# Recurrence outputs and input reloaded earlier, six of eight batches gated and summed before the last batch's feed-forward

## What is computed

```python
xn = layernorm(x)                                  # [8, 256, 128]
s  = recurrence(xn)                                # linear recurrence over the 256 tokens of each batch
y  = xn
for i in range(6):                                 # 6 layers, 16 heads of 64, windows of 32
    y = local_attention(shift(y), Wqkv[i], ...) @ Wo[i] + y
    y = feed_forward(shift(y), ln_g[i], ln_b[i], W1[i], b1[i], W2[i], b2[i]) + y
out = x + s * silu(y)
```

## Time and profile before

| what | value |
|---|---|
| median of 3 runs | 1658.5 us (1656.65 to 1660.97) |
| profiled execution, its own time | 1657.53 us |
| its span, first to last instruction | 1655.7 us (1.83 us less) |
| mean granted TensorE clock | 0.990 of full speed |
| busy share PE / DVE / ACT / POOL | 95% / 86% / 67% / 74% |

### The profile page before, as it was taken

One profiled execution on the slowest core, in us unless ns is written; L12 is line 12 of the kernel. 1 busy time (PEld: TensorE's weight loads), 2 busy tenths in 40 slices (PEclk: granted clock), 3 DMA queues, 4 the chain that ended last, 5 costly groups with the idle time before them and its releaser, 6 DMA issues.

```text
span 1655.7 us, 75427 instructions
## 1 busy us (share of the span) xinstructions
PE 1567.6 (95%) x31996; PEld 1312.3 (79%) x31996; DVE 1416.7 (86%) x2757; ACT 1109.9 (67%) x1980; POOL 1231.0 (74%) x1200
## 2 busy tenths in 40 slices
PE   4889999999999999999999999999999999999995
PEld 2468888788888788888888888888888877888884
DVE  4698899889889988988988898989889888888963
ACT  4265777776677777667776766777676776767663
POOL 2377788878778887877887787787778887777851
PEclk9799999999999999999999999999999999999998
DMA  3033223333223323322333322333323333322222
GB/s 112 22 92 73 66 72 81 92 79 86 69 68 73 101 69 89 74 72 68 93 79 82 82 70 69 94 78 82 82 67 73 84 86 82 83 68 66 71 64 81
DMA packets 109742, 127.96 MB, mean 77 GB/s; under 512 B 52064, under 2 KB 55648, under 8 KB 109152
## 3 DMA queue, kind: packets, MB, share of 16 engines
q1 hardware_dynamic: 109408, 123.13, 29.5%
HBM read 20.27 MB, written 2.10 MB: 14 GB/s over the span
## 4 chain that ended last, share of the span: by engine, by line
PE 62%; DVE 12%; ACT 11%; issue 7%; POOL 6%; DMA 1%; SPq 0%; DVEq 0%; POOLq 0%; ACTq 0%
PE F L529 10%; PE O L634 9%; PE VTb L542 7%; PE S L559 6%; PE QKb L500 6%; PE F L599 4%; PE QKb L502 4%; PE QKb L501 4%; DVE t L882 4%; PE S L580 3%; ACT L773 3%; ACT hid L773 2%; DVE mx L910 2%; POOL t L1052 2%; PE S L552 2%
## 5 line engine op out<-in xcount | busy, mean ns | idle before, releaser
L1052 POOL TENSOR_TENSOR t<-t 128x512 f32<-128x512 f32 x384 | 492.2, 1282 | 193.6 <-DVE t L882 180.4
L882 DVE TENSOR_TENSOR t<-QKb,table 128x1024 f32<-128x1024 f32 x384 | 468.3, 1220 | 61.5 <-ACT sq L713 59.4
L1027 POOL TENSOR_TENSOR t<-t,rn 128x512 f32<-128x512 f32 x384 | 401.3, 1045 | 128.5 <-DVE rn L939 128.4
L713 ACT ACTIVATE sq<-QKb 128x512 f32<-128x512 f32 x384 | 231.2, 602 | 238.0 <-PE QKb L502 232.6
L634 PEld LDWEIGHTS O<-PT,V 64*64 64x64 f32 x12288 | 198.6, 134 | 57.5 <-issue 55.3
L634 PE MATMUL O<-PT,V 64*64 64x32 f32 x12288 | 218.4, 220 | 15.9 <-DVE rn L939 15.8
L891 DVE TENSOR_REDUCE ss<-sq 128x16 f32<-128x1024 f32 x192 | 232.0, 1209 | 0.0
L542 PE MATMUL VTb<-cst,t 128*128 128x128 f32 x1536 | 230.5, 272 | 0.1
L529 PEld LDWEIGHTS F<-wo_sb,OT 128*128 128x128 f32 x1536 | 200.5, 191 | 16.3
L1034 POOL TENSOR_TENSOR E<-E,rs 128x512 f32<-128x512 f32 x192 | 200.4, 1044 | 14.6 <-DVE rs L904 14.6
L542 PEld LDWEIGHTS VTb<-cst,t 128*128 128x128 f32 x1536 | 185.4, 141 | 31.1 <-POOL t L1027 2.8
(11 more groups left out here) (152 smaller groups left out, 2769.3 us busy)
## 6 DMA issues: line engine op xcount, KB each, us to landing
V<-v_tok SPq DMA_DIRECT2D x1440, 64.0 KB, 2.0
w_raw<-in_wqkv SPq DMA_DIRECT2D x36, 256.0 KB, 3.0
wo_sb<-in_wo SPq DMA_DIRECT2D x6, 512.0 KB, 4.1
xs<-xm SPq DMA_DIRECT2D x48, 64.0 KB
xs<-xm SPq DMA_DIRECT2D x48, 63.5 KB
w_sb<-in_w SPq DMA_DIRECT2D x6, 341.0 KB
w_sb<-in_w SPq DMA_DIRECT2D x6, 192.0 KB, 3.8
y_spill<-OT SPq DMA_DIRECT2D x1, 1024.0 KB, 4.2
```

Source lines behind the costliest of these rows:

```text
L713: act.activation(sq[:, v % 4, :], QK_ps, ACT.Square).then_inc(sq_done, 1)
L882: dve.tensor_tensor(t12[:, v:9 + v % 4:8 + v % 4 - v, :].rearrange("p c (h d) -> p c h d", h=8), QK_ps.rearrange("p (h d) -> p h d", h=8). ...
L1027: pool.tensor_tensor(w, w, rn[:, vv // 4, 8 * (vv % 4):8 * (vv % 4 + 1)].unsqueeze(2) .to_broadcast([P, 8, DH]), ALU.mult).then_inc(qk_nor ...
L1052: pool.tensor_tensor(w, w, t12[:, 8 + v % 4, :].rearrange("p (h c d) -> p h c d", h=8, c=2)[:, :, ::-1, :], ALU.add).then_inc(add_done, 1)
```

## The change

The recurrence's output is read back into `sq` and not into `V[:, 1]`, which allows it from slot 4 of step 48 on. The reload of x moves to slot 0 of step 49. ACT applies silu to six batches in slot 2 of step 50, and DVE multiplies and adds these six in slot 5 of step 50, after it has finished batch 6 (step 46). Two batches are left for the end. The transposes stay where they were, and so do all operations in number, except that ACT loads its function table two times more.

```diff
+Y_LOAD, X_LOAD = STEPS * SLOTS + 4, STEPS * SLOTS + 8
+EARLY, GATED, MIXED = B - 2, STEPS * SLOTS + 18, STEPS * SLOTS + 21
 Y_BACK = STEPS * SLOTS + 19
...
-        y_back = V[:, 1, 0:4, :].rearrange("p a b -> p (a b)").rearrange("p (b n) -> p b n", b=B)
+        y_back = sq[:, :, :].rearrange("p a b -> p (a b)").rearrange("p (b n) -> p b n", b=B)
...
+                    if s * SLOTS + v == Y_LOAD:
+
+                        wait(sp, ss_done, UNITS // 2)
+                        wait(sp, y_saved, 16)
+                        sp.dma_start(y_back, y_spill).then_inc(in_y, 16)
+                    if s * SLOTS + v == X_LOAD:
+
+                        wait(sp, o_ready, (STEPS - 1) * QPS)
+                        sp.dma_start(x_tok, x.rearrange("b (t p) d -> p (b t) d", p=P)).then_inc(in_x2, 16)
                     if s * SLOTS + v == Y_SLOT:
...
             all_steps(sp, step)
 
-            sp.wait_ge(y_saved, 16)
-            sp.wait_ge(o_ready, QUADS)
-            sp.dma_start(y_back, y_spill).then_inc(in_y, 16)
-            sp.dma_start(x_tok, x.rearrange("b (t p) d -> p (b t) d", p=P)).then_inc(in_x2, 16)
             for b in range(B):
                 sp.wait_ge(o_done, b + 1)
...
+                    if s * SLOTS + v == GATED:
+                        gate(range(EARLY))
+
+            def gate(batches):
+
+                for b in batches:
+                    act.wait_ge(ff_final, STEPS - B + b + 1)
+                    act.activation(xt[:, b, :, :], xt[:, b, :, :], ACT.Silu).then_inc(g_done, 1)
+
...
             all_steps(act, step)
 
-            for b in range(B):
-                act.wait_ge(ff_final, STEPS - B + b + 1)
-                act.activation(xt[:, b, :, :], xt[:, b, :, :], ACT.Silu).then_inc(g_done, 1)
+            gate(range(EARLY, B))
...
+                    if s * SLOTS + v == MIXED:
+                        mix(range(EARLY))
...
+            def mix(batches):
+
+                dve.wait_ge(yT_ready, 1)
+                dve.wait_ge(in_x2, 16)
+                for b in batches:
+                    dve.wait_ge(g_done, b + 1)
+                    y_ = banks[b // 2][:, N * (b % 2):N * (b % 2 + 1)].rearrange("p (t d) -> p t d", t=NT)
+                    dve.tensor_tensor(xt[:, b, :, :], y_, xt[:, b, :, :], ALU.mult).then_inc(prod_done, 1)
+                    dve.wait_ge(prod_done, b + 1)
+                    dve.tensor_tensor(o_tok[:, NT * b:NT * (b + 1), :], xt[:, b, :, :], x_tok[:, NT * b:NT * (b + 1), :],
+                                      ALU.add).then_inc(o_done, 1)
...
             all_steps(dve, step)
 
-            dve.wait_ge(yT_ready, 1)
-            ...
+            mix(range(EARLY, B))
```

## The result

| | kernel before | kernel changed |
|---|---|---|
| median of 22 runs each | 1658.43 us (1655.95 to 1661.8) | 1655.41 us (1650.84 to 1663.19) |
| ratio of the times | | 0.998, 95% interval 0.9972 to 0.9988 |
| span of the profiled execution | 1655.7 us | 1652.7 us |

The change gains 3.0 us, 0.2% (0.12 to 0.28%). The forecast was 6.5 us. 1655.4 lies within the range, but a gain of this size is less than half the forecast and falls into the case "within 0.3%", to which I had given 0.24.

What follows compares the result with a forecast made beforehand. The end was bound by y_spill's load with its transposes, plus finished batches' arithmetic. An earlier first hid (1.7) and six fewer final pairs (4.76) gave 6.5 us: 1658.5 to 1652.0, range 1649.0 to 1656.5.

Steps and rivals of the forecast that it cites:

- within 0.3%: Outcome in which the whole kernel's time differs by under 0.3%, 5.0 us, from before; chance 0.24.
- The mechanism: At the kernel's end, y's load with transposes and finished batches' arithmetic needlessly lie in the chain; removal gains 6.5 us.
- 6 × 0.794 = 4.76 us less: Behind the last ff_final, two product-and-sum pairs stand instead of eight, saving 4.76 us.
- The transposes of y and the table load: After step 46's W2, 16 transposes take 1.76 us; the 1.28 us load before step 47's gelu costs only 0.10.
- The rival of the tables: Before step 47's first gelu, the table switch costs another 1.28 us beyond its load; gain 6.2, 1652.3 us; chance 0.05.
- The first hid starts at 1640.6: In step 47, the first feed-forward product starts at 1640.6 instead of 1642.33, behind six early pairs: 1.7 us gained.
- the interference between DVE's sums and POOL: In step 47, POOL's normalizing holds DVE's early sums; six pairs end at about 1640.6 instead of 1639.59.
- The clock: After PE's idle time in step 47, the clock falls; W1's third chunk and W2 take 2.5 us more; chance 0.08.
- The two loads, earlier: I take 0: Loads of y before step 47's last value moves and x before step 46's shift cost 0, having queue room.
- the stretch up to 1632.95 moves by more than 1 us: Sign that the whole prediction is wrong: work up to step 46's W2 end, counted as untouched, shifts over 1 us.
- DVE not held: Rival: in step 47, POOL does not hold DVE's early sums; gain 7.5 us, time 1651.0; chance 0.15.

Runs made afterwards that it cites:

- e4: Changed kernel plus 16 filler transposes of the identity on PE behind those of y; 1652.21 us, ratio 0.9963 to the kernel before.
- e3: Changed kernel with both loads early, but all eight silus, products and sums at the end as before; 1658.59 us, ratio 0.9997 to the kernel before.
- e5: e4 with DVE doing the products first and the sums after; 1653.01 us, ratio 0.9972 to the kernel before.
- e8: Changed kernel with y_spill laid out batch by batch, so its load moves 1 KB pieces; 1656.26 us, ratio 0.9991 to the kernel before.
- e6: e5 with the load of y moved behind step 46's shift; 1651.65 us, ratio 0.9963 to the kernel before.
- e10: e6 with the last two batches in pairs of product and sum again; 1649.76 us, ratio 0.9948 to the kernel before.
- e9: Changed kernel once more, unedited, beside e10 on the same chip; 1653.05 us, ratio 0.9973 to the kernel before.
- e7: Kernel before plus one extra, unread load of y_spill into sq ahead of step 47's last value moves; 1661.61 us, ratio 1.0021.

## Why the prediction was right and wrong

*The mechanism: right.* The load of `y_spill` behind the shift and the arithmetic of finished batches were the removable parts; both left the chain. "6 × 0.794 = 4.76 us less" at the end: measured 4.77.

*The transposes of y and the table load: right.* 16 transposes after W2 at the full clock, the end modelled to 1636.52; I had counted 1.76 us from the end of W2 (here 1634.76), and they took that. The load between `xc` and gelu took 1.28 with at most 0.02 on each side. In e4, where W1 was fast, the gelu came 1.88 us behind the start of `xc`; the forecast was 1.89. By the 2.66 for a switch of the Trainium skill's "ScalarE: Activation LUTs", section "What ACT_TABLE_LOAD costs", it would have been 3.2, an estimate; the measurement decides. The rival of the tables fell.

*"The first hid starts at 1640.6": the step that failed, and for another reason than I had.* I had the first `hid` 14.13 us behind `xm`; it came at 14.62 (1642.91), and it waited for ACT's gelu, which waited for W1 at half clock, and not in DVE's queue. Even where the clock stayed up (e4) it waited for ACT, at 13.53. I had `xn`'s transposes 10.28 us behind `xm`; they came at 10.66. I had the interference between DVE's sums and POOL, but with the wrong one suffering: from L854 I took DVE to be held by 0.75 to 1.34 us. DVE's sums took 0.42 us, all six pairs ended 13.11 us behind `xm` (13.12 is what I had worked out without any disturbance), and POOL lost 0.45. e3 and e5 show that the sums are the cause, since without them beside it the pair takes 1.58. The Trainium skill, "GPSIMD Engine Reference", section "1. Specifications", says that SBUF interfaces are shared with VectorE, with contention at instructions with two SBUF inputs. The rows agree, and that section doesn't say who loses; here it was once the one and once the other.

*The clock: a rival that came true.* I gave it 0.08 and a price of 2.5 us. It came in five of six profiles in which PE had the idle time, at 20.17 − 17.88 = 2.29 us. My argument was that before's clock fell after 3.45 us of idleness and that now it was 2.04. The idle time became 2.44 (0.4 of it POOL's), but the size was no argument: in e3 it was 2.01 and the clock fell, in e8 it was 2.44 and it stayed up, and in front of step 45's W2 it fell after 1.58 in five profiles of twelve. With the filler it stayed up in four profiles of four (e4, e5, e6, e10) against one of six without; what decides between falling and not stays open. Whether these falls are why the changed kernel's times spread from 1650.8 to 1663.2 isn't shown either.

*"The two loads, earlier: I take 0": failed.* I asked who stands behind them on SP's queue, and those had room: the shift of step 46 and the value moves are nowhere in the chain. But a load shares the DMA engines with something that isn't in the program's queues, the fetch of instructions. It came 3.4 us late, and PE, which goes through 64 short matmuls in under a us, ran out. PE stood for 0.9 to 1.8 us in all eight profiles that have the load there (in e3 in two pieces, 0.38 and 0.53), and not at all in the three where it is behind the shift. `xm` was 1.82 late in the changed kernel's profile: 1.60 the stall, 0.27 the value product behind it, less 0.06 by which the group had started earlier. The 0.27 has the same look: the next record of q8 starts at 1611.08, and in e3, e5 and e8 the value product, too, goes on 2.65 to 2.71 us behind the start of that record. I had named "the stretch up to 1632.95 moves by more than 1 us" as what would make the prediction wrong, and it did.

Taken together: 6.5 − 1.8 (upstream) − 2.3 (clock) − 0.4 (POOL) + 1.0 (DVE not held) = 3.0. That the time still fell into my range was luck in part: the stall had no term in it at all, the clock's fall was counted alone, and an error of the other sign, DVE not held, gave 1.0 back. That the sum of one pair of profiles is also the difference of the medians is luck as well: e9's profile of the same kernel has a span of 1657.9 us, 2.2 more than before's, with two more falls of the clock far ahead of this stretch and the one under step 45's W2.

## What to carry to other kernels

When a large load is moved to a quieter place, look not only at what is behind it on its queue, but also at the instruction records in the DMA view and at whether an engine with many short instructions runs through there. When PE is freed of work in front of a wait, the short matmuls behind the wait may run at half clock; a filler that takes up most of the wait was free here, and products and sums can be ordered so that those with two SBUF inputs don't lie beside POOL's critical work. Each of the three was worth 0.4 to 2.3 us in the profiles, against a change of 3. And before a profile is compared with another, the granted clock ahead of the stretch should be compared too: a fall that came in one and not in the other was worth 1.6 us.

## What the runs showed of the hardware that I had not expected

- A 1 MB load kept a fetch of instructions waiting: its record came in the us from 1605 and not from 1601, and PE stood still for 1.36 us in the midst of 64 matmuls. With pieces of 1 KB it still stood for 1.21. That the late record is PE's own block is inferred, since the record doesn't name its engine: the two come and go together, and PE goes on 2.5 to 2.8 us behind its start in all eight profiles.
- DVE's operation with two inputs in SBUF, begun just after POOL's, was not held (0.42 us) and made POOL's 0.45 longer, while L854 was itself held. Which of them has to wait is open.
- The granted clock fell after PE had been idle for 2.0 to 2.4 us in five of six profiles, and not in one. It fell after 1.58 us of idleness in five of twelve profiles, and in e7 behind the stall of 1.83 us. The stalls of 0.4 to 1.6 us in the other seven profiles left it at 1.00.
